# Rows 1024 to 1535 of tile 6's transposed context all taken from memory, tile 6's residual kept on the core, eight scans of W2 moved

## The chip, the cores and the metric

One core of one Trainium2 chip runs the whole program in one launch. The metric is the device time of one execution in microseconds (us); lower is better. The kernel before takes 1365.68 us, the median of 3 runs (1365.51 to 1367.25).

## The reference, cut to what matters

16 batches of 64 tokens (N = 1024) attend to a context of 1601 rows per batch; then follow a differential self-attention over the tokens and a feed-forward layer with ternary weights. The change touches the first part, and the place of some scans for the largest absolute weight.

```python
x1 = layernorm(x)                                   # 16 x 64 x 1024
energy = einsum('bcn,bmn->bcm', x1, ctx)            # m: 1601 context rows
attn = softmax(energy, -1); attn /= 1e-9 + attn.sum(axis=1)
x_r = einsum('bcm,bmn->bcn', attn, ctx)
t = x1 - (conv_w @ x_r + conv_b)
x = x + x1 + relu(batchnorm(t))                     # statistics over all 16 batches
x = x + differential_attention(layernorm(x))        # Wq, Wk, Wv, Wo
# ternarize(W): delta = 0.05 * max(abs(W)), for W1 and W2 alike
x = x + fp4(ternary(gelu(ternary(layernorm(x), W1, b1)), W2, b2))
```

## The kernel before, in words

**Context stage.** A tile p (0 to 7) is two batches, 128 tokens. The context of a tile is needed twice: by rows for the weighted sum (`ctx_sb`, 13 row tiles of 1 MB, line 464) and transposed for the energies. Rows 0 to 1023 come transposed from memory in eight chunks of 1 MB (`ctxT`, `load_T`, line 452), through a ring of six slots of 1 MB: a load waits until the use six places earlier in the ring is done (`ctxT_used`). Of rows 1024 to 1535, TensorE makes the transpose itself ("pairs": lines 1040, 1043), ScalarE and VectorE copy it to `stg` (lines 757, 1552), and TensorE multiplies it (line 1061). For tile 6 half of it, chunks 0 to 3, comes from memory as two more ring uses of 1 MB ("wide", from `in_ctxW`), and for tile 7 all of it: two in the ring and two in `stg` ("apart", line 458), with the 65 rows of the tail in `tails` (line 460). `LOADED[p]` is how many of the eight chunks come so. `loaded_energies` (line 1077) multiplies them, `tail_energies` (line 1084) the tail.

TensorE's order for each p is: energies of the first four chunks of tile p+1, the transposed weights of tile p (line 1115), the weighted sum of tile p (`weigh_ctx`, line 1133, 104 matmul passes in eight groups; each group that is done frees its row tiles, `pv_done`), the other chunks of tile p+1, and then its wide chunks and pairs (line 1160 on). Row tiles are loaded in the groups `N_GROUPS`: g0 to g4 are row tiles 8 to 12, g5 is 0 to 3 (4 MB), g6 is 4 and 5, g7 is 6 and 7. Nearly all of these loads stand on one queue, SP's, in the order of the code: a load that waits holds up all behind it. The layernorm of tile p+1 (`make_x1`, line 1514) stands on VectorE between the copies of tile p's pairs, and `put_x1T(p + 1)` transposes it ahead of the last pair's energies.

After its weighted sum a tile's difference `t` (the residual, `x1s`, two slots) goes to memory from ScalarE's queue (line 751) and comes back as `tok` (line 514); tile 7's stays in `x1s`.

**The hand-over.** When tile 7 is done, VectorE scales `xo` (line 1536, from the loads of line 517), makes the last residual, and the batch statistics; then the values are multiplied (line 1203), with `wv_sb` from line 525.

**Scans.** W1 and W2 have 32 tiles each of 512 KB, and VectorE takes the largest absolute value of each (line 1611), from a ring of four slots: a load waits for the scan four places earlier. 40 scans (`SCANS_V`: 32 of W1, 8 of W2) stand in the value stage as `V_SCANS` says, four ahead of the output projection (`n_scan`), and 20 in it, four for each of the tiles 0 to 4.

The quoted lines that a sentence can't say:

```python
def load_T(q, chunks, kind="chunk"):
    for c in chunks:
        k = RING_NO[(q, kind, c)]
        if k >= SLOTS:
            sp.wait_ge(ctxT_used, USE_NO[RING_USES[k - SLOTS]] + 1)
```

## Time and profile before

| | us |
|---|---|
| median of 3 runs | 1365.68 |
| the profiled execution, its own time | 1365.15 |
| its span, first to last instruction | 1363.3 |
| context stage, to the end of tile 7's weighted sum | 471.3 |
| value stage, from the first transposes of line 1194 | 481.5 to 600.4 |
| queries, keys and heads | 600.4 to 827.9 |
| output projection | 827.9 to 946.4 |
| feed-forward and output | from there to 1363.3 |
| TensorE busy | 1321.5 (97%) |
| VectorE busy | 867.5 (64%) |

The span is what lies between the first and the last instruction; the execution's own time has 1.85 us more around it. TensorE (PE) is busy nearly throughout; its ends are modelled, so that says where it has no gap, not that it is at its peak. The DMA engines are busy through the whole context stage, and at 20 to 90% after it. Stretches in the trace are in us from the span's start.

### The profile page before, as it was taken

To read this page: it belongs to the slowest core of one execution; us is meant where nothing else is said; L and a number is where in the kernel's file an instruction comes from. 1 tells how busy PE (TensorE), PEld (TensorE's weight loads), DVE (VectorE), ACT (ScalarE), POOL (GpSimd) and SP (SyncE) were. 2 spreads that over 40 slices of the span, in tenths; PEclk is the share of its full clock that TensorE was granted. 3 is DMA by queue.
4 is the path that set the end of the run, shared out by engine and by line. 5 is a ranking of instruction groups with operands and counts; after the bars stand their busy time and mean duration, and the time that the engine had idled before them with its cause. 6 is when DMAs were issued, how large, how long until landed. Compare 5 with 4: busy or idle time off the path is not lost.

```text
span 1363.3 us, 17544 instructions
## 1 busy us (share of the span) xinstructions
PE 1321.5 (97%) x6738; PEld 642.8 (47%) x6738; DVE 867.5 (64%) x1470; ACT 486.5 (36%) x751; POOL 2.4 (0%) x10
## 2 busy tenths in 40 slices
PE   6999999999999889999999999999999999999995
PEld 4554646444353344444555555445444444444442
DVE  2332424224231379868899986876999997777974
ACT  1111302112020022127777784112555455444432
POOL 0000000000000000000000000000000000000000
PEclk9999999999999989999999999999999999999997
DMA  9999999999999989916656669452477775222264
GB/s 380 419 420 420 420 421 421 422 420 420 406 406 420 412 330 331 325 30 186 173 149 182 170 200 329 148 211 87 168 259 239 231 263 190 77 77 74 78 182 154
DMA packets 142210, 363.05 MB, mean 266 GB/s; under 512 B 63152, under 2 KB 89904, under 8 KB 115760
## 3 DMA queue, kind: packets, MB, share of 16 engines
q1 hardware_dynamic: 138960, 350.39, 70.2%
q10 hardware_dynamic: 3168, 11.54, 2.1%
q8 instruction: 55, 0.90, 0.3%
q14 instruction: 27, 0.22, 0.0%
HBM read 315.22 MB, written 46.66 MB: 265 GB/s over the span
## 4 chain that ended last, share of the span: by engine, by line
PE 79%; issue 14%; DMA 4%; DVE 2%; ACT 0%; DVEq 0%; POOLq 0%; POOL 0%; ACTq 0%
PE ps L1249 14%; PE ps L1133 12%; PE ps L1405 9%; PE ps L1203 8%; PE ps L1316 8%; PE ps L1023 7%; PE ps L1365 6%; PE ps L1061 4%; PE ps L1043 2%; DMA ctxT<-in_ctxT 2%; PE ps L1115 2%; PE ps L1040 1%; PE ps L1269 1%; DMA xo<-in_x 1%; DMA x_t<-in_x 1%
## 5 line engine op out<-in xcount | busy, mean ns | idle before, releaser
L1454 PE MATMUL ps<-t_half,hl 128*128 128x512 f16 x896 | 193.5, 379 | 0.0
L1133 PE MATMUL ps<-ctx_sb,attnT 128*64 128x512 f32 (+1 forms) x832 | 180.3, 593 | 0.0
L757 ACT ACTIVATE stg<-ps 128x512 f32<-128x512 f32 (+1 forms) x66 | 36.3, 552 | 297.5 <-PE ps L1043 169.1
L1454 PEld LDWEIGHTS ps<-t_half,hl 128*128 128x128 f16 x896 | 87.7, 98 | 105.7
L1023 PE MATMUL ps<-ctxT,x1T 128*64 128x512 f32 x512 | 114.9, 596 | 0.4 <-DMA ctxT<-in_ctxT 0.4
L933 ACT ACTIVATE hl<-hb,al 128x512 f16<-128x512 f32 x112 | 79.2, 720 | 97.5 <-PE ps L1454 83.7
L1133 PEld LDWEIGHTS ps<-ctx_sb,attnT 128*64 128x64 f32 (+1 forms) x832 | 59.0, 137 | 115.3 <-issue 107.9
L1972 DVE SCALAR_TENSOR_TENSOR hl<-hb,al,hl 128x512 f16<-128x512 f32 x112 | 81.9, 749 | 48.7 <-ACT hl L933 48.5
L1203 PE MATMUL ps<-wv_sb,x2T 128*128 128x512 f32 x256 | 112.2, 596 | 0.0
L1316 PE MATMUL ps<-wo_sb,oT 128*128 128x512 f32 x256 | 111.6, 593 | 0.3 <-ACT oT L839 0.3
L1527 DVE SCALAR_TENSOR_TENSOR x1s<-ps,sw,x1s 128x512 f32<-128x512 f32 x16 | 12.0, 749 | 133.1 <-PE ps L1133 133.1
L1552 DVE COPY stg<-ps 128x512 f32<-128x512 f32 (+1 forms) x66 | 41.6, 635 | 69.6 <-PE ps L1043 43.0
L1249 PE MATMUL ps<-xs,tw 128*128 128x512 f32 x192 | 85.0, 592 | 0.0
L1611 DVE TENSOR_REDUCE wmx<-w_scan 128x1 f32<-128x1024 f32 x64 | 74.8, 1212 | 15.2 <-DMA w_scan<-in_w1t 12.4
L1203 PEld LDWEIGHTS ps<-wv_sb,x2T 128*128 128x128 f32 x256 | 48.4, 192 | 58.3 <-issue 58.3
L1316 PEld LDWEIGHTS ps<-wo_sb,oT 128*128 128x128 f32 x256 | 47.9, 190 | 57.6 <-issue 56.9
L1023 PEld LDWEIGHTS ps<-ctxT,x1T 128*64 128x64 f32 x512 | 38.3, 137 | 64.0 <-issue 61.5
L1061 PE MATMUL ps<-stg,x1T 128*64 128x128 f32 (+2 forms) x816 | 59.9, 297 | 0.0
L1249 PEld LDWEIGHTS ps<-xs,tw 128*128 128x128 f32 x192 | 35.9, 190 | 42.6 <-issue 41.1
L1061 PEld LDWEIGHTS ps<-stg,x1T 128*64 128x64 f32 x816 | 40.7, 139 | 11.1 <-issue 8.3
L1365 PE MATMUL ps<-x3h,pieces 128*128 128x512 f16 x192 | 45.4, 379 | 0.0
L1365 PE MATMUL ps<-x3l,pieces 128*128 128x512 f16 x192 | 45.4, 379 | 0.0
(227 smaller groups left out, 1803.7 us busy)
## 6 DMA issues: line engine op xcount, KB each, us to landing
ctxT<-in_ctxT SPq DMA_DIRECT2D x64, 1024.0 KB, 21.9
ctx_sb<-in_ctx SPq DMA_DIRECT2D x40, 1024.0 KB, 20.1
ctx_sb<-in_ctx SPq DMA_DIRECT2D x8, 4096.0 KB, 27.6
ctx_sb<-in_ctx SPq DMA_DIRECT2D x16, 2048.0 KB, 31.6
w_scan<-in_w1t SPq DMA_DIRECT2D x32, 512.0 KB, 6.3
w_buf<-in_w1t SPq DMA_DIRECT2D x32, 512.0 KB, 3.9
w_scan<-in_w2t SPq DMA_DIRECT2D x32, 512.0 KB, 5.0
w_buf<-in_w2t SPq DMA_DIRECT2D x32, 512.0 KB, 4.7
```

The source lines that it names most:

```text
L933: A(hl[:, r % RING, 0, :], hs(LEFT[m], k), ACT.Copy, scale=al[:, 3:4]).then_inc(hi_ready, 1)
L1023: ins = mm(bank(ea + g, m1 - m0)[C * b:C * b + C, :], x1T[:, q % 2, c, C * b:C * b + C], slot((q, "chunk", c))[:, b, m0:m1], start=(c == 0 ...
L1061: ins = mm(out[C * b:C * b + C, :], x1T[:, p % 2, c, C * b:C * b + C], stg[:, e % 4, b, i * w:i * w + w], start=(c == 0), stop=(c == NC - 1))
L1133: ins = mm(bank(ea + hf)[C * b:C * b + C, :], attnT[0:w, slots[mt], C * b:C * b + C], ctx_sb[0:w, mt, b, hf * BANK:hf * BANK + BANK], star ...
L1203: ins = mm(bank(2 * (t % 2) + hf), x2T[:, c, t * P:t * P + P], wv_sb[:, c, hf * BANK:hf * BANK + BANK], start=(c == 0), stop=(c == NC - 1))
L1249: ins = mm(bank(b), right, left, start=(fresh and c == 0), stop=(c == 3), skip_group_check=not fresh)
L1316: ins = mm(bank(2 * (t % 2) + hf), oT[:, c, t * P:t * P + P], wo_sb[:, c, hf * BANK:hf * BANK + BANK], start=(c == 0), stop=(c == H - 1))
L1365: ins = mm(bank(b), left[c // 4][:, c % 4 * P:c % 4 * P + P], part[:, c, j * BANK:j * BANK + BANK], start=(c == 0 and n == 0), stop=(c == ...
L1405: ins = mm(bank(b), left[:, c * P:c * P + P], x3_factor(m, n)[:, c, :], start=(fresh and c == 0 and n == 0), stop=(c == 3 and n == 1), ski ...
L1454: ins = mm(bank(b), hl[:, r % RING, n, s * P:s * P + P], t_half[:, r % BRING, :], start=(fresh and k == 0 and n == 0), stop=(k == HK - 1 a ...
L1611: V.tensor_reduce(wmx[:, n // WT, n % WT:n % WT + 1], buf[:, n % 4, :], AX.X, ALU.max, apply_absolute_value=True).then_inc(scanned, 1)
L1972: V.scalar_tensor_tensor(hl[:, r % RING, 1, :], left(r // HK, r % HK), al[:, 3:4], hl[:, r % RING, 0, :], ALU.mult, ALU.subtract).then_inc ...
```

## The change

Tile 6 takes all eight chunks of rows 1024 to 1535 from memory (`LOADED[6]` 4 to 8), so its four wide pairs go and two ring uses of 1 MB come. The loads of the row tiles and chunks on SP's queue are put in another order while tile 5's weighted sum and tile 6's energies run, and g5 is loaded in two halves. Tile 6's residual isn't stored and read back: `relu` takes it from `x1s`. The eight scans of W2 in the value stage go to the output projection, which has five a tile instead of four. SP's loads for them move with them.

```diff
--- before.py
+++ after.py
@@ -56,7 +56,7 @@
 U = len(UNITS)
 
 SINGLES = [(mt, half) for mt in range(TM, MT) for half in range(2)]
-LOADED = (0,) * (NT - 2) + (4, NC)
+LOADED = (0,) * (NT - 3) + (0, 8, NC)
 
 
 def pairs(p):
@@ -73,7 +73,7 @@
 
 def slots_of_tile(p):
 
-    ring = [(p, "chunk", c) for c in range(NC)] + [(p, "wide", i) for i in range(min(LOADED[p] // 2, 2))]
+    ring = [(p, "chunk", c) for c in range(NC)] + [(p, "wide", i) for i in range(LOADED[p] // 2 if p < NT - 1 else 2)]
     return ring if p < NT - 1 else ring + [(p, "apart", i) for i in range(2)]
 
 
@@ -88,8 +88,8 @@
 HC = HID // P
 WT = HID * N // P // 1024
 WH = WT // H
-SCANS_V = 40
-V_SCANS = (0, 0, 2, 6, 7, 7, 7, 7, 4)
+SCANS_V = 32
+V_SCANS = (0, 0, 1, 5, 6, 6, 7, 7, 0)
 EPS = 1e-5
 LAMBDA_INIT = 0.8 - 0.6 * math.exp(-0.3 * 12)
 X_SCALE = 512.0
@@ -459,8 +459,14 @@
                 for i in range(2):
                     sp.dma_start(tails[i][:, :, :, :], ctxE_in[i]).then_inc(apart_got, 16)
 
-            def load_N(q, g):
+            def load_N(q, g, part=None):
                 m0, m1 = N_GROUPS[g][0], N_GROUPS[g][-1] + 1
+                if g == 5 and part is None:
+                    load_N(q, g, 0)
+                    load_N(q, g, 1)
+                    return
+                if g == 5:
+                    m0, m1 = 2 * part, 2 * part + 2
                 sp.dma_start(ctx_sb[:, m0:m1, :, :], ctx[q, m0 * P:m1 * P].rearrange("(t p) b n -> p t b n", p=P))\
                   .then_inc(ctx_in[g], 16)
 
@@ -480,10 +486,10 @@
             load_T(1, range(4, 6))
             for p in range(NT - 1):
 
-                def next_N(groups):
+                def next_N(groups, part=None):
                     for g in groups:
                         sp.wait_ge(pv_done, G * p + g + 1)
-                        load_N(p + 1, g)
+                        load_N(p + 1, g, part)
 
                 load_T(p + 1, range(6, 7))
                 if p + 1 < BY_ROW:
@@ -493,6 +499,23 @@
                 else:
                     load_T(p + 1, range(7, NC))
                     load_T(p + 1, range(min(LOADED[p + 1] // 2, 2)), "wide")
+                    if LOADED[p + 1] and p + 1 < NT - 1:
+                        if LOADED[p + 1] == 4:
+                            next_N(range(0, 5))
+                            next_N((5,), 0)
+                            load_T(p + 2, range(0, 4))
+                            next_N((5,), 1)
+                        else:
+                            next_N((4, 0, 1))
+                            load_T(p + 1, range(2, 4), "wide")
+                            next_N((2,))
+                            load_T(p + 2, range(0, 2))
+                            next_N((3,))
+                            load_T(p + 2, range(2, 4))
+                            next_N((5,))
+                        next_N(range(6, G))
+                        load_T(p + 2, range(4, 6))
+                        continue
                     if p + 1 == NT - 1:
                         load_apart()
                         next_N((5, 7, 0, 1, 2, 6, 3, 4))
@@ -501,9 +524,9 @@
                 if p == 0:
                     sp.dma_start(lam_sb[:, 0:4 * D], lambdas.partition_broadcast(P)).then_inc(lam_in, 16)
                 if p + 2 < NT:
-                    load_T(p + 2, range(0, 4 if p < 2 or LOADED[p + 1] else 2))
+                    load_T(p + 2, range(0, 4 if p < 2 else 2))
                 next_N(range(5, 6))
-                if p >= 2 and p + 2 < NT and not LOADED[p + 1]:
+                if p >= 2 and p + 2 < NT:
                     load_T(p + 2, range(2, 4))
                 next_N(range(6, G))
                 if p + 2 < NT:
@@ -517,13 +540,13 @@
                 sp.dma_start(xo[:, t0:t1, :], x_v[t0:t1].rearrange("t p n -> p t n")).then_inc(s, 16)
 
             sp.wait_ge(ctxT_used, len(USES))
-            sp.wait_ge(n_stored, 16 * (NT - 1))
+            sp.wait_ge(n_stored, 16 * (NT - 2))
             load_tok(0, 2)
             sp.wait_ge(pv_done, G * NT - 7)
             load_xo(0, 2, s_in[0])
             sp.wait_ge(pv_done, G * NT - 3)
             sp.dma_start(wv_sb[:, :, :], wv.rearrange("(c p) n -> p c n", p=P)).then_inc(wv_in, 16)
-            load_tok(2, NT - 1)
+            load_tok(2, NT - 2)
             load_xo(2, NT, s_in[1])
             sp.wait_ge(pv_done, G * NT)
 
@@ -546,7 +569,7 @@
                 scan_load(n, w_scan)
                 if n == 8:
                     load_qk(1)
-                if n == 34:
+                if n == 28:
                     sp.wait_ge(xs_ready, 6)
                     load_qk(0)
                 if n == 24:
@@ -746,7 +769,7 @@
             put_x1T(0)
             load_x(1)
             for p in range(NT):
-                if p:
+                if 1 <= p < NT - 1:
                     act.wait_ge(cv_free, 2 * p)
                     act.dma_start(n_dram[p - 1], x1s[:, (p - 1) % 2, :]).then_inc(n_stored, 16)
                 for e, pair in enumerate(pairs(p)):
@@ -757,7 +780,7 @@
                     A(stg[:, e % 4, 0, 0:n], bank(pair_bank(p, e, 0), n), ACT.Copy).then_inc(act_tr_out, 1)
                     if e == (2 if not LOADED[p] else 0) and p + 1 < NT:
                         sqrt(p + 2, slice(0, 1))
-                    if e == 8 and p + 2 < NT:
+                    if e == min(8, len(pairs(p)) - 1) and p + 2 < NT:
                         load_x(p + 2)
                 if p + 1 < NT:
                     put_x1T(p + 1)
@@ -775,7 +798,7 @@
             act.wait_ge(bn_ready, 2)
 
             def relu(t):
-                src = tok[:, t, :] if t < NT - 1 else x1s[:, 1, :]
+                src = tok[:, t, :] if t < NT - 2 else x1s[:, t % 2, :]
                 A(tok[:, t, :], src, ACT.Relu, bias=bnm[:, 7:8], scale=bnm[:, 6:7]).then_inc(relu_done, 1)
 
             def put_v(t, hf):
@@ -1027,7 +1050,7 @@
             def pair_transposes(p, e):
                 kind, a = pairs(p)[e]
                 n = pair_no(p, e)
-                for g in [e // 2] if e % 2 == 0 and p < BY_ROW else range(4) if e == 0 else [4] if e == len(pairs(p)) - 2 else []:
+                for g in [e // 2] if e % 2 == 0 and p < BY_ROW else [4] if e == len(pairs(p)) - 2 else range(4) if e == 0 else []:
                     pe.wait_ge(ctx_in[g], 16 * p + 16)
                 if e == 0 and p:
                     pe.wait_ge(at_out, U * p)
@@ -1128,7 +1151,7 @@
                         w = width(mt)
                         pe.wait_ge(at_out, U * p + 1 + next(u for u, mts in enumerate(units) if mt in mts))
                         g = next(k for k, mts in enumerate(N_GROUPS) if mt in mts)
-                        pe.wait_ge(ctx_in[g], 16 * (p + 1))
+                        pe.wait_ge(ctx_in[g], (32 if g == 5 else 16) * (p + 1))
                         for b in range(2):
                             ins = mm(bank(ea + hf)[C * b:C * b + C, :], attnT[0:w, slots[mt], C * b:C * b + C],
                                      ctx_sb[0:w, mt, b, hf * BANK:hf * BANK + BANK], start=(mt == order[0]), stop=(mt == order[-1]))
@@ -1160,15 +1183,15 @@
                 weigh_ctx(p)
                 if p + 1 < NT and LOADED[p + 1]:
                     chunk_energies(p + 1, range(4, NC))
-                    if p == 5:
-                        loaded_energies(6)
-                        two(pair_transposes, 6, 0)
-                        two(pair_transposes, 6, 2)
-                        two(pair_energies, 6, 0)
-                        later_pairs(6)
+                    loaded_energies(p + 1)
+                    if p + 1 < NT - 1:
+                        two(pair_transposes, p + 1, 0)
+                        if len(pairs(p + 1)) > 2:
+                            two(pair_transposes, p + 1, 2)
+                            two(pair_energies, p + 1, 0)
+                        later_pairs(p + 1)
                     else:
-                        loaded_energies(7)
-                        tail_energies(7)
+                        tail_energies(p + 1)
                 elif p + 1 < NT:
                     chunk_energies(p + 1, range(4, NC - 1))
                     two(pair_transposes, p + 1, 0)
@@ -1550,10 +1573,10 @@
                         V.wait_ge(e_done, first_pair(p) + e - 3)
                     V.wait_ge(dve_tr, pair_no(p, e) + 1)
                     V.tensor_copy(stg[:, e % 4, 1, 0:n], bank(pair_bank(p, e, 1), n)).then_inc(dve_tr_out, 1)
-                    if e == len(pairs(p)) - 3:
+                    if e == max(len(pairs(p)) - 3, 0):
                         V.wait_ge(ctxT_used, used_by(p))
                         own.done(V.tensor_reduce(mx4[:, 0:1], ps[:, ea * BANK:(ea + 2) * BANK], AX.X, ALU.max))
-                    if e == len(pairs(p)) - 5 and p + 1 < NT:
+                    if e == max(len(pairs(p)) - 5, 0) and p + 1 < NT:
                         make_x1(p + 1)
                 if p < NT - 1:
                     V.wait_ge(e_done, first_pair(p + 1) - 2)
@@ -1929,7 +1952,7 @@
                     t_low(4, 0)
                     t_sums(4, 1)
                     t_low(4, 1)
-                for _ in range(4):
+                for _ in range(5):
                     if n_scan < 2 * WT:
                         scan(n_scan, w_scan2)
                         n_scan += 1
```

What the new order on **SP** is at the place in question: `in_ctx` are row tiles, `in_ctxT` chunks, `in_ctxW` wide chunks. Before, from the last chunks of tile 6 (the first row) to those of tile 7:

```order
L452 DMA ctxT<-in_ctxT 128x2048 [waits ctxT_used] x4
L452 DMA ctxT<-in_ctxW 128x2048 [waits ctxT_used] x2
L464 DMA ctx_sb<-in_ctx 128x2048 [waits pv_done] x5
L452 DMA ctxT<-in_ctxT 128x2048 [waits ctxT_used] x4
L464 DMA ctx_sb<-in_ctx 128x4x2048 [waits pv_done]
L464 DMA ctx_sb<-in_ctx 128x2x2048 [waits pv_done] x2
L452 DMA ctxT<-in_ctxT 128x2048 [waits ctxT_used] x4
```

and with the change:

```order
L452 DMA ctxT<-in_ctxT 128x2048 [waits ctxT_used] x4
L452 DMA ctxT<-in_ctxW 128x2048 [waits ctxT_used] x2
L470 DMA ctx_sb<-in_ctx 128x2048 [waits pv_done] x3
L452 DMA ctxT<-in_ctxW 128x2048 [waits ctxT_used] x2
L470 DMA ctx_sb<-in_ctx 128x2048 [waits pv_done]
L452 DMA ctxT<-in_ctxT 128x2048 [waits ctxT_used] x2
L470 DMA ctx_sb<-in_ctx 128x2048 [waits pv_done]
L452 DMA ctxT<-in_ctxT 128x2048 [waits ctxT_used] x2
L470 DMA ctx_sb<-in_ctx 128x2x2048 [waits pv_done]
L470 DMA ctx_sb<-in_ctx 128x2x2048
L470 DMA ctx_sb<-in_ctx 128x2x2048 [waits pv_done] x2
```

Five row tiles stood together, ahead of tile 7's chunks; now three stand there (g4, g0, g1), then the two new wide loads, and g2 and g3 come one at a time behind them.

On **PE**, from tile 6's last four chunks to the energies of its tail, before:

```order
L1023 MATMUL ps<-ctxT,x1T 64x512 x16
L1077 MATMUL ps<-ctxT,x1T 64x512 x8
L1040 MATMUL ps<-cst,ctx_sb 128x128 x32
L1061 MATMUL ps<-stg,x1T 64x512 x4
L1043 MATMUL ps<-cst,ctx_sb 128x65 x16
L1061 MATMUL ps<-stg,x1T 64x512 x4
L1006 MATMUL ps<-cst,x1s 128x128 x8
L1061 MATMUL ps<-stg,x1T 64x65 x16
```

and with the change:

```order
L1046 MATMUL ps<-ctxT,x1T 64x512 x16
L1100 MATMUL ps<-ctxT,x1T 64x512 x16
L1066 MATMUL ps<-cst,ctx_sb 128x65 x16
L1029 MATMUL ps<-cst,x1s 128x128 x8
L1084 MATMUL ps<-stg,x1T 64x65 x16
```

The 32 transposes are gone, their eight energy matmuls come out of `ctxT`, and the transpose of tile 7's `x1s` now directly follows the tail's transposes.

## Rows read from the trace of the kernel before

**Rows 1.** The page's part 2, 40 equal slices of the span.
```profile
DMA  9999999999999989916656669452477775222264
GB/s 380 419 420 420 420 421 421 422 420 420 406 406 420 412 330 331 325 30 186 173 149 182 170 200 329 148 211 87 168 259 239 231 263 190 77 77 74 78 182 154
```

**Rows 2.** Stretches of 10 us: busy us (x instructions) by engine, PEclk, DMA share, GB/s.
```profile
360.00:370.00 10.00, 10.00 (x50) 3.39 (x48) 0.00 (x0) 0.00 (x0) 0.00 (x0) 1.00 1.01 421
370.00:380.00 10.00, 10.00 (x49) 3.29 (x46) 4.44 (x8) 0.00 (x0) 0.00 (x0) 1.00 0.86 313
```

**Rows 3.** The chain that ended last, by time: start us, us, what.
```profile
371.72 6.87 PE ps L1023 x32
378.58 3.43 PE ps L1077 x16
...
393.43 7.06 PE ps L1023 x32
...
455.93 13.24 DMA xo<-in_x
481.49 1.97 PE ps L1194 x8
```

**Rows 4.** The timeline of SP's queue: start us, us of issuing, what.
```profile
358.02 0.33 SPq L464 DMA_DIRECT2D ctx_sb<-in_ctx  x1
373.48 5.48 SPq L452 DMA_DIRECT2D ctxT<-in_ctxT  x4
379.00 1.73 SPq L464 DMA_DIRECT2D ctx_sb<-in_ctx  x3
```

**Rows 5.** DMA issues begun at 358.02, 373.48, 379.00, 436.2: count, KB, us to landing.
```profile
ctx_sb<-in_ctx SPq DMA_DIRECT2D x1, 1024.0 KB, 18.1
...
ctxT<-in_ctxT SPq DMA_DIRECT2D x1, 1024.0 KB, 6.9
...
ctx_sb<-in_ctx SPq DMA_DIRECT2D x1, 4096.0 KB, 19.8
...
ctx_sb<-in_ctx SPq DMA_DIRECT2D x1, 1024.0 KB, 27.7
```

**Rows 6.** DMA issues of the whole run: count, KB each, median us to landing.
```profile
w_scan<-in_w2t SPq DMA_DIRECT2D x32, 512.0 KB, 5.0
t_half<-t_dram SPq DMA_DIRECT2D x112, 128.0 KB, 2.0
...
wqk_a<-in_wqk SPq DMA_DIRECT2D x4, 1024.0 KB, 6.3
```

**Rows 7.** The timeline at the end of the context stage.
```profile
469.26 0.81 DVE L1536 TENSOR_SCALAR xo<-xo,rr 128x1024 f32<-128x1024 f32 x1 [18.30 <-DMA xo<-in_x]
469.45 1.89 PE L1133 MATMUL ps<-ctx_sb,attnT 128*64 128x512 f32 x8
...
471.50 0.73 DVE L1527 SCALAR_TENSOR_TENSOR x1s<-ps,sw,x1s 128x512 f32<-128x512 f32 x1
```

**Rows 8.** Groups by line from 371.7 to 393.4 us (busy us, mean ns, idle before).
```profile
L1040 PE MATMUL ps<-cst,ctx_sb 128*128 128x128 f32 x32 | 3.9, 276 | 0.6 <-ACT stg L757 0.6
...
L1552 DVE COPY stg<-ps 128x512 f32<-128x512 f32 (+1 forms) x6 | 3.5, 601 | 8.8 <-PE ps L1040 8.5 <-PE ps L1043 0.3
...
L1555 DVE TENSOR_REDUCE mx<-ps 128x1 f32<-128x1024 f32 x1 | 1.2, 1215 | 0.0
...
L1514 DVE TENSOR_SCALAR x1s<-x_t,mv,rr 128x1024 f32<-128x1024 f32 x1 | 0.8, 812 | 0.0
```

**Rows 9.** Two stretches of one tile's length, value stage and output projection.
```profile
578.93:593.54 14.61, 14.61 (x42) 6.96 (x41) 14.54 (x22) 2.17 (x4) 0.00 (x0) 1.00 0.11 45
857.21:871.82 14.61, 14.61 (x36) 6.48 (x35) 13.30 (x28) 0.41 (x2) 0.00 (x0) 1.00 0.42 143
```

**Rows 10.** The timeline of the output projection.
```profile
862.59 4.59 DVE L1611 TENSOR_REDUCE wmx<-w_scan 128x1 f32<-128x1024 f32 x4
867.10 1.28 DVE L1913 TENSOR_TENSOR xr<-ps,xr 128x512 f32<-128x512 f32 x2
...
874.24 8.32 PE L1316 MATMUL ps<-wo_sb,oT 128*128 128x512 f32 x19
```

## The prediction

> **What bounds the kernel now.** I read the page's slices first, then stretches of 10 us, then the chain, and then, for the stretch that the change touches, each DMA issue with its time to landing.
>
> The slices [rows 1] show the DMA engines full from the start to the fourteenth slice, about 477 us, at 420 GB/s; this is the context stage. TensorE is busy in it too, so both have to be asked. In stretches of 10 us [rows 2] the DMA engines move 421 GB/s, and there is one hole in the whole stage: from 370 to 380 us only 313 GB/s, a loss of (421 - 313)/421 x 10 = 2.6 us. The reader is to see that the engines are a line of work without gaps from 380 us to the end of the stage: what is put into that line, or moved behind the hole, comes out at its end.
>
> The chain [rows 3] shows where the end is read. It goes through TensorE until 455.93, and then through the load of `xo`, issued at 455.93 and landed 13.24 later, at 469.17. VectorE starts on `xo` at 469.26 after 18.3 us of idling; the weighted sum of tile 7 ends at 469.45 + 1.89 = 471.34, and the last residual starts at 471.50 [rows 7]. From 469.26 VectorE's own work (scale, first half, its statistics) takes 2.24 us, so it would have started at 471.50 with or without TensorE: the two paths end within 0.2 us of each other. A microsecond won by TensorE alone is worth nothing here, and a microsecond lost by the DMA line counts in full: the value stage, which starts at 481.49, hangs on it, and from there on TensorE has no gap of note (14.61 busy of 14.61 in the stretches shown [rows 9]).
>
> **What the change does to TensorE.** It takes away 32 transposes, 3.9 us, and 0.6 us of idling before them [rows 8]; the energies only change their source. That is 4.5 us at most of the 21.7 us from 371.72 to 393.43 [rows 3]. But VectorE makes tile 7's `x1s` between its copies, and in the new order nothing stands between the tail's transposes and the transpose of `x1s`. One copy (0.6), the maximum (1.2) and `x1s` (0.8) [rows 8] and, as an estimate of the size of a copy, the root now come in series, about 3.1 us. I take 4.5 - 3.1 = 1.4 us won on TensorE.
>
> **What it does to the DMA line.** One MB is 1.049e6 bytes; at 421 GB/s it takes 2.49 us. Loads land in the order of issue: the 4 MB load issued at 379.00 lands at 398.8, those after it in steps of that rate, the last row tile at 436.2 + 27.7 = 463.9 and `xo` at 469.17 [rows 3 to 5].
>
> *The hole.* Before, five row tiles are issued while the weighted sum of tile 5 runs; the last at 358.02 lands at 358.02 + 18.1 = 376.1. Tile 7's first chunk can't be issued before chunk 4 of tile 6 is used, 373.48, and lands 6.9 later, at 380.4 [rows 4, 5]. Now only three row tiles are issued ahead of it, so the line is through at 376.1 - 2 x 2.49 = 371.1. The next load, the first new wide chunk, needs that same ring slot and so still waits until 373.5; g2 and g3, whose places in `ctx_sb` have long been free, stand behind it. The wide chunk finds an empty line: the nearest row for 1 MB alone is 6.3 us [rows 6], so it lands at 379.8. Behind it, ahead of the end of g5, lie one wide chunk, g2, g3, four chunks and the 4 MB of g5: 11 MB, 27.4 us, so 407.2. Before, g5 landed at 398.8. **+8.4 us**, of which 5.0 are the two new MB and 3.4 the two row tiles moved behind the hole.
>
> *The store.* Tile 6's residual is no longer written: 0.5 MB less ahead of `xo`, 0.524e6/421e3 = **-1.25 us**. The 0.5 MB read less stands behind `wv` and is off the path.
>
> *The rest of the line* is the same work without a gap, so `xo` lands at 469.17 + 8.4 - 1.25 = 476.3, **+7.15 us**. The last row tile lands at 471.05; behind its arrival TensorE has 12 of the 104 passes left, at 1.89 us for eight [rows 7] 2.8 us, so it ends near 473.9, still ahead of the residual at 471.50 + 7.15 = 478.65. So TensorE's 1.4 us are not seen.
>
> Bounds of the hole: from below, the smallest time to landing in the run is 2.0 us (128 KB) [rows 6]; with that the wide chunk lands at 373.5 + 2.0 + 2.5 = 378.0, 1.8 earlier, and the sum is +5.3. From above, the line runs once more as thinly as in the stretch of 313 GB/s, 2.6 us more, +9.7. I take +7.15, since the 6.3 us row is the same size and the same queue.
>
> The Trainium skill, DMA: Bandwidth & Descriptors, section Anatomy of one DMA, gives a fixed 2.0 us for one transfer beside its bytes; by it the sum is the +5.3 of the lower bound. No row here shows that for 1 MB: the lone loads of that size take 6.3 us.
>
> The rate is the row's 421 GB/s. The same page, section Where 436 GB/s comes from, has the HBM side bind at about 358 GB/s per core for such loads. By that 1.5 MB net would cost 4.4 us and not 3.7, and the sum would be about 1.6 us higher; the trace is above that figure through the whole stage, so the measurement decides.
>
> **What else it touches.** In the value stage VectorE is busy 14.54 of 14.61 us in its fullest tile [rows 9], TensorE has no gap; eight scans less there win nothing. In the output projection VectorE does 13.30 in the first tile, four scans (4.59) among them, and now five. The ring has four slots, so the fifth waits for a load that is issued when the first scan is done: 862.59 + 1.2 + 5.0 = 868.8 [rows 6, 10], and with the scan itself 870.0. The sums that stood at 867.10 then end at 871.3. TensorE needs them at 874.24 [rows 10]: 2.9 us are left, and more in the later tiles, where TensorE's 14.6 us a tile outlast VectorE's. I cost it at nothing; the cover is those 2.9 us.
>
> **The sum.** 1365.15 + 7.15 = 1372.3 on the profiled execution. The median of the runs is 0.5 above that execution; I take half of it, **1372.5 us**.
>
> **The rivals.**
> *Only the bytes count.* The line catches up with the moved row tiles, since the engines have work enough later; +2 MB - 0.5 MB is +3.7 us, 1369.1. For it: the hole of now costs only 2.6 us. Against: from 380 us on there is no room in which to catch up.
> *The other side: TensorE decides.* If `xo` and tile 7's last row tiles have slack that I don't see (if `xo` doesn't wait for the line, but for its own long issue), the 1.4 us of TensorE come through: 1364.0; with the chain on VectorE hidden as well, 4.5 us, 1360.9. It decides once the line's delay at `xo` is under 0.2 us. Against: VectorE's wait of 18.3 us is for that very load.
> *The output projection is late too.* If the fifth scan's load takes over 8 us and not 5.0, the sums miss 874.24, and each tile behind may add to it; some 2 us on top, 1374.5.
> That the change doesn't do what it says is ruled out by the order of its instructions.
>
> **How the numbers follow.** A difference under 0.2%, 2.7 us, is about what can't be told from none. Main forecast, 5.3 to 9.7 us slower: 0.66. Bytes only: 0.12, also slower. Output projection on top: 0.06, slower. TensorE decides: 0.16, of which 0.11 within 0.2% and 0.05 faster. So 0.84 slower, 0.11 the same, 0.05 faster. The range takes in the main case (1370.5 to 1375.4), the bytes alone with room for the runs' spread, and the third rival: 1368.0 to 1376.0. It leaves out the 0.16 of the second.
>
> **What would show each step.** In the new trace: a hole in the DMA share between about 369 and 375 us, deeper than the 0.86 of now; g5 of tile 6 landing 8 us later; `xo` landing near 476; VectorE's residual waiting on `xo`, with tile 7's weighted sum ended 3 to 5 us before it; the value stage starting near 488.6; the same length from there to the end. I am wrong if `xo` lands before 472, if the weighted sum of tile 7 ends last, or if a gap shows on TensorE after 860 us.

## The result, and the profile after

The change makes the kernel slower: 1374.31 us, the median of 5 runs (1371.59 to 1374.86), against 1365.95 (1365.51 to 1367.25, 5 runs) for the kernel before on the same chip. The ratio is 1.0055 [1.0043, 1.0066], which is 7.5 us where the medians differ by 8.4. The prediction was 1372.5 in 1368.0 to 1376.0, with 0.84 on slower. All medians here are over every execution, of which one each in e5, e7, e8 and e10 took 2010 us or more; the ratios leave these four out.

The profiled execution is the one of 1374.31 us; its span is 1372.4, 9.1 above the 1363.3 of before. Line numbers from `load_N` on are higher by 6 and those of the programs of TensorE, VectorE and ScalarE by 23 (L1023 is now L1046).

The slices of the page answer to [rows 1]:

```profile
DMA  9999999999899988705665669554486775222254
GB/s 377 419 421 420 421 421 420 423 420 421 337 415 420 417 340 278 290 23 163 168 172 152 188 178 323 212 203 173 159 275 223 243 266 191 77 77 77 77 175 159
```

The eleventh slice falls to 337 GB/s, and no other slice of the stage moves by over 10. The stretches answer to [rows 2]; the first one below lies ahead of them, and the last two of 2 us lie in the hole:

```profile
358.00:360.00 2.00, 2.00 (x12) 0.61 (x10) 0.00 (x0) 0.00 (x0) 0.00 (x0) 1.00 0.74 287
...
360.00:370.00 10.00, 10.00 (x50) 3.39 (x48) 0.00 (x0) 0.00 (x0) 0.00 (x0) 1.00 0.87 360
370.00:380.00 10.00, 10.00 (x48) 3.29 (x46) 4.44 (x8) 0.00 (x0) 0.00 (x0) 1.00 0.60 198
380.00:390.00 10.00, 7.46 (x46) 2.93 (x42) 2.62 (x7) 2.15 (x4) 0.00 (x0) 0.98 1.01 421
...
370.00:372.00 2.00, 2.00 (x12) 0.59 (x10) 1.06 (x2) 0.00 (x0) 0.00 (x0) 1.00 0.13 49
372.00:374.00 2.00, 2.00 (x12) 0.69 (x10) 1.73 (x3) 0.00 (x0) 0.00 (x0) 1.00 0.00 0
```

TensorE is busy for all of 360 to 380 us while the DMA engines run dry and, from 372 to 374, move nothing. The 313 GB/s of before is now 198. SP's timeline says why, and answers to [rows 4]:

```profile
358.88 1.28 SPq L470 DMA_DIRECT2D ctx_sb<-in_ctx  x3
374.33 2.04 SPq L452 DMA_DIRECT2D ctxT<-in_ctxW  x2
376.42 0.43 SPq L470 DMA_DIRECT2D ctx_sb<-in_ctx  x1
377.77 2.04 SPq L452 DMA_DIRECT2D ctxT<-in_ctxT  x2
379.86 0.44 SPq L470 DMA_DIRECT2D ctx_sb<-in_ctx  x1
```

SP issues nothing between 360.2 and 374.33. The row tiles g2 and g3 leave at 376.42 and 379.86, behind the wide chunks. There is a second, shallow hole, at 358 to 362 us (287 and 369 GB/s, where before has 426 and no dip): in the new order g4 stands first, it waits for the fifth group of tile 5's weighted sum, and so the first row tile leaves at 358.88, where before it left at 351.15. The times to landing answer to [rows 5]; here that of the first wide chunk, issued into the empty line, and that of `xo` at the other end, issued at 459.53:

```profile
ctxT<-in_ctxW SPq DMA_DIRECT2D x1, 1024.0 KB, 6.2
...
xo<-in_x SPq DMA_DIRECT2D x1, 1024.0 KB, 17.7
```

The end of the context stage on VectorE, answering to [rows 7], and the value stage's start on TensorE:

```profile
477.29 0.81 DVE L1559 TENSOR_SCALAR xo<-xo,rr 128x1024 f32<-128x1024 f32 x1 [22.73 <-DMA xo<-in_x]
478.14 0.75 DVE L1550 SCALAR_TENSOR_TENSOR x1s<-ps,sw,x1s 128x512 f32<-128x512 f32 x1
...
452.40 22.60 PE L1156 MATMUL ps<-ctx_sb,attnT 128*64 128x512 f32 x104
...
489.73 1.97 PE ps L1217 x8
491.69 8.90 PE ps L1226 x16
```

`xo` is here the input of the token tiles 0 and 1 (`load_xo(0, 2)`), which the value stage takes first. VectorE waits 22.73 us for it, where it waited 18.30. The weighted sum of tile 7 has been done since 452.40 + 22.60 = 475.00, 3.1 us before the residual that reads it starts. The value stage starts at 489.73, 8.24 later than before.

**Where the 9.1 us of span came from.** The two profiled executions differ by 0.86 already at 228 us, ahead of the new order: there TensorE waits for a chunk whose landing was at 200.53 + 27.62 = 228.15 before and is at 200.62 + 28.40 = 229.02 now. Of the change only the halves of g5 stand ahead of it, in every tile. In the seven traces that have them (the change among them) the landing lies between 227.33 and 229.46, and in the three that don't between 228.15 and 228.62, so the halves show no cost there, and I take the 0.86 for scatter and measure from that landing. `xo` lands 469.17 - 228.15 = 241.02 later in the one, and 477.19 - 229.02 = 248.17 later in the other: **+7.15**. From the value stage's start to the end it is 881.81 before and 882.67 now, 0.86 more; the first 16 passes alone take 8.90 where they took 7.98. The rest, 0.2, lies between `xo` and the value stage.

### The profile page after: what moved, and what is told of

The parts are those of the page before. It is cut to its first block, busy times and chain, and to the rows that moved or that the text cites. A ratio compares the mean times of both kernels' runs of the same rounds, so it can differ in the third digit from the quotient of the medians.

```text
span 1372.4 us, 17467 instructions
## 1 busy us (share of the span) xinstructions
PE 1320.8 (96%) x6706; PEld 639.2 (47%) x6706; DVE 865.1 (63%) x1466; ACT 484.3 (35%) x747; POOL 2.4 (0%) x10
## 4 chain that ended last, share of the span: by engine, by line
PE 73%; issue 14%; DMA 8%; DVE 2%; SPq 1%; ACT 0%; DVEq 0%; POOLq 0%; POOL 0%; ACTq 0%
PE ps L1272 14%; PE ps L1156 10%; PE ps L1428 9%; PE ps L1226 8%; PE ps L1339 8%; PE ps L1388 6%; PE ps L1046 6%; DMA ctxT<-in_ctxT 5%; PE ps L1084 3%; PE ps L1138 2%; DMA tail<-in_ctxE 2%; PE ps L1066 1%; DMA xo<-in_x 1%; PE ps L1063 1%; PE ps L1292 1%
## 5 line engine op out<-in xcount | busy, mean ns | idle before, releaser
L1046 PE MATMUL ps<-ctxT,x1T 128*64 128x512 f32 x512 | 116.9, 601 | 1.8 <-DMA ctxT<-in_ctxT 1.7
L1046 PEld LDWEIGHTS ps<-ctxT,x1T 128*64 128x64 f32 x512 | 37.5, 139 | 68.1 <-issue 61.1
L1084 PE MATMUL ps<-stg,x1T 128*64 128x128 f32 (+2 forms) x800 | 55.9, 291 | 0.0
L1066 PE MATMUL ps<-cst,ctx_sb 128*128 128x128 f32 (+1 forms) x368 | 41.9, 268 | 2.3 <-DMA ctx_sb<-in_ctx 1.5
```

The source lines that it names most:

```text
L1046: ins = mm(bank(ea + g, m1 - m0)[C * b:C * b + C, :], x1T[:, q % 2, c, C * b:C * b + C], slot((q, "chunk", c))[:, b, m0:m1], start=(c == 0 ...
L1084: ins = mm(out[C * b:C * b + C, :], x1T[:, p % 2, c, C * b:C * b + C], stg[:, e % 4, b, i * w:i * w + w], start=(c == 0), stop=(c == NC - 1))
```

## The experiments

The theory: `xo` is the gate of the value stage, and comes later by the added bytes and by the row tiles moved behind the hole. (Two of the expectations call it `xo` of tile 6; the load and the scale that they mean are those of the token tiles 0 and 1.) The rivals: the bytes alone; a cost of the scans; the new wait on TensorE; and, once the trace was read, the order on VectorE, which holds tile 7's finished residual behind `xo`.

In the table, "start" is the value stage's start less the landing of the early chunk, both in the profiled execution, as above. Each ratio is to the kernel before, run beside it on the same chip, with medians of 1365.3 to 1366.0.

| kernel | median, us | ratio to before | start, us |
|---|---|---|---|
| before | 1365.95 | | 253.34 |
| the change | 1374.31 | 1.0055 [1.0043, 1.0066] | 260.71 |
| e1, g2 and g3 early | 1368.63 | 1.0019 [1.001, 1.0028] | 257.42 |
| e2, one more MB | 1375.56 | 1.0071 [1.0058, 1.0083] | 262.77 |
| e3, before with the scans moved | 1365.69 | 0.9999 [0.999, 1.0008] | 252.11 |
| e4, before with 640 KB for row tile 12 | 1390.19 | 1.0184 [1.0167, 1.02] | |
| e5, residual first | 1369.54 | 1.0029 [1.0018, 1.0039] | |
| e6, e1 and e5 together | 1365.31 | 0.9997 [0.9988, 1.0006] | 252.77 |
| e7, `x1s` early | 1373.79 | 1.0056 [1.0043, 1.007] | 261.15 |
| e8, three wide chunks and the edits of e1, e5, e7 | 1362.80 | 0.9978 [0.9969, 0.9988] | 250.88 |
| e9, before, residual first | 1365.51 | 0.9999 [0.999, 1.0009] | 253.37 |
| e10, e5 again | 1369.54 | 1.0029 [1.0017, 1.0042] | 257.48 |

### e1: the row tiles back ahead of the hole

```diff
-                            next_N((4, 0, 1))
+                            next_N((4, 0, 1, 2, 3))
                             load_T(p + 1, range(2, 4), "wide")
-                            next_N((2,))
-                            load_T(p + 2, range(0, 2))
-                            next_N((3,))
-                            load_T(p + 2, range(2, 4))
+                            load_T(p + 2, range(0, 4))
```

> The changed kernel with one edit: the row tiles g2 and g3 of tile 6 stand ahead of the two new wide loads again. Theory (the DMA line decides, and 3.4 us of its delay are the two row tiles moved behind the hole): the hole gets shallower, xo lands about 3.4 us earlier than in the changed kernel (477.2 to about 473.8), and the time falls from 1374.3 to about 1370.9, still about 5 us above before. Rival (only the bytes count, the order doesn't): 1374.3, no difference. Rival (TensorE decides): no difference, or later, since the wide loads now land behind the row tiles.

Measured: 1368.63. The hole is back to less than that of before, and VectorE gets `xo` at 472.32:

```profile
370.00:380.00 10.00, 10.00 (x50) 3.29 (x47) 3.69 (x7) 0.00 (x0) 0.00 (x0) 1.00 0.92 347
...
472.32 0.81 DVE L1556 TENSOR_SCALAR xo<-xo,rr 128x1024 f32<-128x1024 f32 x1 [22.60 <-DMA xo<-in_x]
```

From the early chunk's landing (227.33), `xo` lands 244.89 later (454.70 + 17.52 = 472.22): 3.3 less than with the change, and 3.87 more than before. The first number answers to the prediction's 3.4 for two row tiles moved behind the hole, the second to its 3.7 for 1.5 MB net. Both halves of the theory's sum are there, to within the 1 us or so by which single traces differ (e3). The kernel still loses 2.8 us, and "bytes only" is what is left of the change without the move.

The time itself was a miss: 1370.9 was expected, a fall of 3.4, and the median fell by 5.7 (4.9 by the ratios). Between the two profiled executions, 4.81 apart, 1.69 lie ahead of the early chunk's landing, where the two kernels are the same. Why the whole time gained more than `xo` did isn't shown.

### e2: one more MB behind the hole

```diff
                             load_T(p + 2, range(0, 2))
+                            sp.wait_ge(e_done, first_pair(NT - 2))
+                            sp.dma_start(stg[:, 2:4, :, :], ctxW_in[NT - 1, 0]).then_inc(apart_got, 16)
                             next_N((3,))
```

A 1 MB load that nobody reads; the two waits on its semaphore are adapted.

> The changed kernel with one load of 1 MB more, into a half of stg that is free, behind the hole; nobody uses it. Theory (the DMA line decides): xo lands 2.5 us later, at about 479.7, and the time is 1376.8. Rival (TensorE decides, the line has slack): 1374.3, unchanged.

Measured: 1375.56, 1.25 above the change, and `xo` lands at 463.29 + 16.14 = 479.43, which is 250.23 from the early chunk (229.20), or 2.06 more than with the change. A MB is 2.49 us, so nearly all of what is put into the line behind the hole comes out at `xo`; the 0.4 in between is less than the scatter of one trace. The time missed the 1376.8 expected: the median rose by half of the 2.5, the ratio by 0.16%, or 2.2 us, and the intervals of the two ratios overlap. The landing shows the step better than the time does.

### e3: the scans alone

```diff
-SCANS_V = 40
-V_SCANS = (0, 0, 2, 6, 7, 7, 7, 7, 4)
+SCANS_V = 32
+V_SCANS = (0, 0, 1, 5, 6, 6, 7, 7, 0)
...
-                for _ in range(4):
+                for _ in range(5):
```

> The kernel before with the move of the eight scans alone (32 in the value stage, five a tile in the output projection). Theory: nothing, 1365.9 within 0.5; TensorE without a gap in both stages; VectorE waits some 1 to 2 us for the fifth scan's load in each tile. Rival (the output projection gets late): about 2 us slower, with a gap on TensorE after 860 us. Rival (fewer scans help the value stage): faster.

Measured: 1365.69, ratio 0.9999. The scans cost nothing and win nothing. The load of `wqk_b` that hangs on the number of the scan is moved with them. The trace of the change shows the first five that follow each other:

```profile
871.74 5.95 DVE L1634 TENSOR_REDUCE wmx<-w_scan 128x1 f32<-128x1024 f32 x5
877.61 1.28 DVE L1936 TENSOR_TENSOR xr<-ps,xr 128x512 f32<-128x512 f32 x2
```

5.95 us for five is 1.19 each: the fifth did not wait, and behind it no scan of the output projection waits over 0.4 us, where 1 to 2 were expected. A load of such a scan, issued near 873 us, landed 3.5 us after its issue where I had taken 5.0. TensorE has no new gap behind 860 us. This run also shows the scatter of a single trace: `xo` landed 239.78 after the early chunk, 1.24 less than before, with not a byte changed in that stage. The 7.15 of the change is to be read with about such an uncertainty.

### e4: fewer bytes, a miss

In the kernel before, row tile 12 holds 65 rows in use, and its load fetches 128. This run loads 80 of them, 640 KB for 1 MB, for each of the eight tiles.

```diff
+                if g == 4:
+                    sp.dma_start(ctx_sb[0:80, m0:m1, :, :], ctx[q, m0 * P:m0 * P + 80].rearrange("(t p) b n -> p t b n", p=80))\
+                      .then_inc(ctx_in[g], 16)
+                    return
```

> The kernel before with the last row tile (65 of 128 rows used) loaded as 80 rows: 0.375 MB less a tile, 3 MB in all, 0.9 us of them behind the hole. Theory (both paths end together in the kernel before): xo lands at least 0.9 us earlier, but TensorE's weighted sum then ends last, so at most 0.2 us are won there; with the small waits for chunks near 50 and 228 us up to 1 us: 1365.0 to 1365.9. Rival (the DMA line alone sets the end of the stage): 1365.9 less 0.9 to 7.5.

Measured: 1390.19, 24.4 us slower than the kernel before beside it (1365.81), where it should have been no slower. The windows show a full line that moves less; first the rows of before for the same 60 us, then those of this run:

```profile
300.00:360.00 60.00, 59.94 (x358) 27.61 (x356) 19.54 (x46) 10.74 (x18) 0.00 (x0) 1.00 1.01 421
```

```profile
300.00:360.00 60.00, 58.11 (x349) 27.01 (x346) 19.54 (x46) 10.74 (x18) 0.00 (x0) 1.00 1.01 394
...
ctxT<-in_ctxT SPq DMA_DIRECT2D x64, 1024.0 KB, 26.2
...
ctx_sb<-in_ctx SPq DMA_DIRECT2D x8, 640.0 KB, 28.2
```

The share is 1.01 in both, at 421 and at 394 GB/s. The chunks take 26.2 to landing for 21.9 before. So a load of 80 partitions occupies the line longer than one of 128. As an estimate it is 24.4 / 8, about 3 us more for each, with 0.4 MB less in it; the estimate puts the whole loss on the eight loads. That the time follows the DMA line is confirmed from the other side, since TensorE now waits 10.6 us for chunks (0.4 before) and VectorE 28.25 us for `xo`; that the line is counted in bytes holds only for loads of one shape. Why the narrow load is dear was not separated.

### e5 and e10: the residual of tile 7 ahead of xo

```diff
-            both(0)
             residual(NT - 1)
...
             V.bn_aggr(bnm[:, 0:2], bn[:, :, :, :].rearrange("p a b n -> p (a b n)")).then_inc(bn_part, 1)
+            both(0)
```

> The changed kernel with VectorE's scale of xo (which waits for the load of xo) moved behind tile 7's residual and the collecting of the statistics. Theory (the stage ends on VectorE's wait for xo at the end of the DMA line, while tile 7's weighted sum ended at 475.0): the residual starts at about 475.2, the scale at 477.3, and the value stage some 3.5 us earlier: 1374.3 to about 1370.8. Rival (TensorE's weighted sum sets the end): no difference.

Measured: 1369.54, where 1370.8 was expected. e10 is the same kernel, and its trace is the one shown.

> The change with residual first once more, for its trace. Theory: time 1369.5 again; xo of tile 6 lands near 477 as in the change, the two residual halves are done before it (near 471.5), and the value stage starts near 485, some 5 us earlier than the change's 489.73, the rest of the loss being xo's own lateness with the gate behind it. Rival: the residual halves wait for TensorE's last eviction as before and the value stage starts no earlier than 488.

Measured: 1369.54 again, 4.8 us below the change with the same loads. VectorE in e10:

```profile
476.72 0.75 DVE L1550 SCALAR_TENSOR_TENSOR x1s<-ps,sw,x1s 128x512 f32<-128x512 f32 x1 [0.17 <-PE ps L1156]
...
478.24 0.59 DVE L1682 BATCH_NORM_AGGREGATE bnm<-bn 128x2 f32<-128x96 f32 x1
478.74 0.74 DVE L1559 TENSOR_SCALAR xo<-xo,rr 128x1024 f32<-128x1024 f32 x1
```

`xo` has landed (461.26 + 16.2 = 477.5) before VectorE comes to it and costs no wait. But the start is 486.94 and not the 485 expected, since the residual now waits for TensorE, whose weighted sum ends at 476.70 and not near 471. Half of that expectation failed: the order is worth 3.2 us of start (260.71 to 257.48), and the other 4.1 of the loss stand, because TensorE hangs on the same line. Where before has no wait, it waits 2.54 us for the tail's load in e10, and runs the 16 passes behind in 5.12 us for the 3.60 of before, with a granted clock of 0.50 from 440 to 442 us:

```profile
440.00 5.12 PE L1100 MATMUL ps<-stg,x1T 128*64 128x512 f32 x16 [2.54 <-DMA tail<-in_ctxE]
```

Together that is 2.54 + 1.52 = 4.06.

### e6: both repairs

The edits of e1 and e5 in one kernel.

> Both edits on the changed kernel: the two row tiles ahead of the wide loads again, and the scale of xo behind the residual. Theory: the two gains add, 1368.6 less 3.5, about 1365.1, level with before; the value stage then also nears the landing of wv. Rival (the hole and xo are the same 3 to 4 us): 1368.6.

Measured: 1365.31, ratio 0.9997: the whole loss of the change is gone, with its two added MB and its other edits in place.

```profile
471.00 0.75 DVE L1547 SCALAR_TENSOR_TENSOR x1s<-ps,sw,x1s 128x512 f32<-128x512 f32 x1 [0.17 <-PE ps L1153]
...
473.02 0.74 DVE L1556 TENSOR_SCALAR xo<-xo,rr 128x1024 f32<-128x1024 f32 x1
```

The residual waits for TensorE alone, and the scale of `xo` for nothing. So what e1 still lost, 2.8 us of the median with `xo` 3.87 late, is gone once the finished residual no longer stands behind `xo`.

### e7: x1s ahead of the tail's copies

VectorE makes tile 7's `x1s` and the maximum before tile 6's last two copies, and ScalarE its root earlier:

```diff
...
+                if p == NT - 2:
+                    make_x1(p + 1)
+                    V.wait_ge(ctxT_used, used_by(p))
+                    own.done(V.tensor_reduce(mx4[:, 0:1], ps[:, ea * BANK:(ea + 2) * BANK], AX.X, ALU.max))
                 for e, pair in enumerate(pairs(p)):
...
```

> The changed kernel with tile 7's x1s (its root on ScalarE, and the maximum) made ahead of the copies of tile 6's tail, so TensorE has no wait of 3 us before its transposes. Theory (the line decides): TensorE's wait at 387 to 390 us is gone, it waits for loads instead, and the time stays at 1374.3 within 0.5. Rival (TensorE decides and VectorE's series ate the gain): 3 us faster, 1371.3.

Measured: 1373.79, no gain over the change's 1374.31 that can be told. TensorE's 3 us wait is gone, and other waits stand in its place, here those from 340 to 480 us:

```profile
PE ps L1048 <- DMA ctxT<-in_ctxT: 3.8, 2, 3.4
PE ps L1102 <- DMA tail<-in_ctxE: 3.6, 1, 3.6
```

In the change these two are none and 1.6 over the same stretch. Of two limits in parallel, shortening the one that isn't last buys a wait.

### e8: one wide chunk less, with the three edits

`LOADED` of tile 6 is 6 and not 8: three wide chunks of 1 MB, for the four of the change and the two of before, and so one added MB in place of two. The edits of e1, e5 and e7 are in it.

```diff
-LOADED = (0,) * (NT - 3) + (0, 8, NC)
+LOADED = (0,) * (NT - 3) + (0, 6, NC)
```

> A version to beat both: tile 6 takes six of eight chunks from memory (1 MB less than the change), row tiles ahead of the wide loads, x1s early, residual first. Theory: line and TensorE in balance, tile 7's weighted sum ends near 469 to 470, xo lands near 470.4, the scale no longer holds up the residual; 1 to 2 us faster than before, 1364.3. If TensorE's part is wrong: level with e6.

Measured: 1362.80, ratio 0.9978 [0.9969, 0.9988], 3 us faster than the kernel before and 11 than the change. The weighted sum of tile 7 ends at 445.53 + 22.54 = 468.07, `xo` costs no wait, and the start is the earliest of all. Both ends were expected a little later (469 to 470, 1364.3). It was measured as a whole: what the fewer chunks, the early `x1s` and the orders each give of the 3 us was not separated beyond e6.

### e9: the kernel before, residual first

> The kernel before with the residual halves of tile 7 ahead of the gate and xo of tile 6 on VectorE, as in the earlier residual run. Theory: there nothing waits for xo long, because TensorE's weighted sum of tile 7 (469.45+1.89) and the residual halves (to 471.50) end within a fraction of a microsecond of the late work after xo (469.26), so the order on VectorE is worth at most its two idle steps: 1364.5 to 1366.5, the same as before. Rival: the order is worth its 5 us everywhere, also without the hole: then 1361.

The edit is that of e5. Measured: 1365.51, ratio 0.9999, start 253.37 for 253.34. The order on VectorE is worth nothing where `xo` and TensorE end together, and 4.8 us of the median (3.6 by the ratios) where `xo` comes late. So the gain of e8 isn't the order's alone.

## Why the prediction was right

**The hole.** As said: thin from 368 us and dry from 372 to 374, the next load at 374.33 (373.5, and 0.86 of offset), landing 6.2 later where 6.3 was taken. The fixed 2.0 us of a transfer that the Trainium skill gives (DMA: Bandwidth & Descriptors, section Anatomy of one DMA), for loads that GpSimd issues, would with 2.5 for the bytes be 4.5, as an estimate; this trace has 6.2 for a lone MB from SP's queue, so the measurement decides, and the sum's lower bound was rightly not taken.

**The term of g5.** Its second half is issued at 383.77 and, as two loads of 20.3 and on average 22.6 us to landing show, lands 24.9 later, at 408.7. Less the offset that is +9.0 over the 398.8 of before, for the 8.4 predicted. The prediction left out the shallow hole at 358 to 362 us: it took the first row tile to leave as before, while g4's wait holds it to 358.88. At the 406, 287 and 369 GB/s of the three stretches of 2 us from 356 on, that is an estimated 0.95 us of a line of 421, about the 0.6 that is over. The two parts of the term are borne out by e1: 3.3 for the moved row tiles (3.4 said), and 3.87 for the bytes net of the store (3.7 said).

**The sum.** +7.15 at `xo`, for +7.15 predicted. The agreement to the last digit is luck: +9.0 at g5 less the store's 1.25 would be 7.75. More traces have the same loads, and in them `xo` lands 241.0, 239.8 and 239.7 us behind the early chunk (before, e3, e9), and 248.2, 248.6 and 248.0 (the change, e7, e10). The means differ by 8.1, inside the 5.3 to 9.7 of the main case and 1 us above its sum, which is about the estimate for the shallow hole. e1 and e6, with 244.9 and 244.2, split it into 3.7 for the moved row tiles and 4.4 for the bytes.

**Bytes only**, the first rival, fell with e1: it is true of a kernel in which g2 and g3 aren't moved. **TensorE decides** fell with the trace, where VectorE waits 22.73 us for `xo`, and with e7, which frees TensorE of its wait and wins nothing. **The output projection** fell with e3 and with the scans there, none of which waits over 0.4 us.

**TensorE's end.** The weighted sum of tile 7 was said to end at 473.9, and ends at 475.00, less the offset 474.1. The number is right and the way to it isn't: it was to wait for the last row tile, but its 104 passes run through in 22.60 us (22.54 before). It ends late because it starts late: tile 6's transposed weights, two steps ahead, are 0.98 behind before's (402.26 for 400.42, less the offset), after the stretch at half the clock, and the tail's load adds a wait of 1.62.

**Two sizes that were off.** TensorE's 1.4 us won didn't come at all: from the last chunks of tile 6 to the first of tile 7 are 394.41 - 372.57 = 21.84 us, where they were 21.71 [rows 3]; by the timelines of e1 and e10, 0.4 and 0.8 us of it came. The series on VectorE was as estimated, 3.05 for 3.1, but behind it TensorE ran at half its clock, which the step left out. It cost nothing, being off the path; in e10, where the residual goes first, TensorE's lateness counts. And "the same length from there to the end" missed 0.86 us, for the same reason. This, the 0.86 that the execution had lost ahead of the new order and the 0.2 behind `xo` are the 2 us between 1372.3 and the profiled 1374.31.

**What the prediction didn't see** is that about half of the loss needs the order on VectorE too. It named the two paths that end within 0.2 us, but took the order as given: `xo` late holds back a residual that has been ready for 3 us. Two conditions met, the late load and the work queued behind its wait, and taking away either one gives back about half of the loss or more: 5.7 us of 8.4 by e1 and 4.8 by e5, or by the ratios 4.9 and 3.6 of 7.5.

## What to carry to other kernels

Where a transfer line is full, look for the point at which it runs dry, and ask of each load that an edit moves whether it passes that point: a load with its destination free, queued behind one that waits for a ring slot, is lost bandwidth for all that follow. Where an engine waits on the last transfer of a stage, look at what stands behind the wait in its order; work that doesn't need the transfer goes ahead of it, which costs nothing and makes the stage tolerant of a late load. And shortening the engine beside a full line turns into waits for it, until bytes go or the hole closes.

## What the runs showed of the hardware

**The price of a short wait is more than the wait, and it varies.** In the change, TensorE idles 3.05 us for `x1s` from 387.5 us on. Stretches of 4 us around it, with the clock as the last number but two:

```profile
384.00:388.00 4.00, 3.46 (x28) 1.64 (x24) 0.94 (x2) 1.18 (x2) 0.00 (x0) 1.00 1.01 426
388.00:392.00 4.00, 1.49 (x7) 1.50 (x8) 3.06 (x8) 1.31 (x4) 0.00 (x0) 0.70 1.01 426
392.00:396.00 4.00, 4.00 (x41) 2.44 (x41) 1.08 (x3) 2.63 (x4) 0.00 (x0) 0.50 1.01 424
```

The granted clock falls to 0.50, the 1.2 GHz level, and the work behind the wait is stretched; the same instructions in the two timelines, change first:

```profile
390.51 1.97 PE L1029 MATMUL ps<-cst,x1s 128*128 128x128 f32 x8 [3.05 <-DVE x1s L1537]
392.41 2.00 PE L1084 MATMUL ps<-stg,x1T 128*64 128x65 f32 x32
```

```profile
391.25 1.10 PE L1006 MATMUL ps<-cst,x1s 128*128 128x128 f32 x8
392.28 1.15 PE L1061 MATMUL ps<-stg,x1T 128*64 128x65 f32 x32
```

That is 0.87 and 0.85 us, and the 32 passes behind take 7.95 for 7.06: with 3.05 of waiting some 5.7 us, more than the 4.5 of work and idling that was taken away. It isn't a fixed price. The same 72 matmuls behind the same wait of 3.05 us, up to the start of the next group, take 9.17 us before, 11.75 in the change, 10.37 in e1 and 10.55 in e10, so the wait costs 2.6, 1.2 and 1.4 us on top of itself. What sets which one isn't shown. At the value stage the gap behind tile 7's weighted sum, with two small matmuls in it, grew from 10.1 to 14.7 us, and the first 16 passes from 7.98 to 8.90 (e1, with 14.6 us, 9.13; e10, with 10.2, 7.99). The gap alone doesn't give the time: e7 has a gap of 13.6 us and takes 7.84, e2 has 13.3 and takes 8.17. The Trainium skill (TensorE: Matmul & The Clock Gate, Part 1) describes the two levels, 1.2 and 2.4 GHz, set by how busy the engine has been, and this trace agrees: 0.50 in the stretch behind the wait, 1.00 ahead of it.

**A narrow load is dearer than a full one.** 80 partitions for 128, at the same 8 KB each, cost an estimated 3 us more a load (e4: 24.4 us over eight loads). The Trainium skill (SBUF — State Buffer, section Door 1: The DMA port swizzle) has the bandwidth depend on the ports that the partitions reach, and the first 64 partitions share half of them. By that, as an estimate, a load of 80 takes as long as the full one and saves nothing; the run shows it to be worse than that, and by what is open.
